# A graph network kernel: every second tile of gathered rows is copied into PSUM and the edge product is added to it there

## The chip, the cores and the metric

The kernel runs on one core of one Trainium2 chip. The metric is the device time of one execution in microseconds (us). A core has five engines with a queue of instructions each: TensorE (PE in the rows; its weight loads are PEld), VectorE (DVE), ScalarE (ACT), GpSimd (POOL) and SyncE (SP), which issues the plain DMA transfers. The engines meet only at semaphores: an instruction that waits holds back everything behind it on its engine.

## What is computed

Two layers of message passing over the same graph of 1250 nodes and 21250 edges, sorted by destination, with 512 features. What matters here is the edge part of each layer:

```python
# layer 0, edge attributes 64 wide
msg  = relu(x[src] + edge_attr @ W_e + b_e)
aggr = segment_sum(msg, dst, num_segments=N)
# layer 1, edge attributes 128 wide
m_in = concatenate([h[src], edge_attr], axis=1)
m    = relu(m_in @ W1.T + b1)
agg  = segment_sum(m, dst)        # @ W2.T + deg * b2 follow on the nodes
```

Layer 0 then has a two-layer perceptron with batch norms over the nodes, layer 1 a gated unit; both end in a layer norm. In layer 1 the node half of `W1` is applied once per node into a table, so that both layers gather ready rows and add an edge product.

## The kernel before

The edges are cut into 167 tiles of 128, in chunks of 4 tiles (one load of edge attributes) and groups of 12 tiles (one window of 128 destination nodes in which the edges of the group fall). One tile passes through the engines in this way, with L the layer and t = u the tile (`JOIN` is 1):

- GpSimd, `gather` (line 415): an indirect DMA fetches the 128 source rows of 512 floats (256 KB) into `raw`, a ring of `RAW` = 8 buffers. The buffer is free when VectorE has made the low part of tile t - 8. The first 12 tiles of layer 0 read `x` itself; later ones read `xb_dram`, x plus the bias, which VectorE makes in five pieces (`make_xb`) and SyncE writes out.
- TensorE, `edge_product` (line 510): two passes in layer 0 and three in layer 1 (the numbers are split into a high and a low part of reduced precision) give the edge product in one of `EDGE_BANKS` = 4 banks of PSUM.
- VectorE, `add_products` (line 1030): `raw` = bank + `raw`.
- ScalarE, `message_high` (line 819): Relu of `raw`, rounded, into `msg_hi`, a ring of `MSG` = 4.
- VectorE, `low_messages` (line 1018): max(`raw`, 0) - `msg_hi` into `msg_lo`, two tiles after the add.
- TensorE, `sum_product` (lines 525, 526): the one-hot matrix `hot` of the destinations times both parts, summed over a group in one of two sum banks, four tiles after the edge product. In layer 1 also the degrees (line 539).

Per chunk, ScalarE copies the attributes, rounded (`high_features`, line 794), VectorE makes their low part (`low_features`, line 949) and the one-hots (`one_hots`, line 1010). Per group, ScalarE copies the sum bank out (`copy_window`, line 794), TensorE transposes it into `turn_bank` (line 550) and VectorE adds it into `agg` (`add_window`, line 1044; degrees at line 1050).

The order on each engine is that of a loop written out by hand, `edges(L)`, one for each engine. ScalarE's loop has the features ahead of the message, the message being the only work of a tile:

```python
while chunk < min(CHUNKS, chunks_in(u + 1) + 1):
    high_features(L, chunk)
    chunk += 1
...
if u < UNITS:
    message_high(L, u)
```

VectorE's loop has for each u: the add of tile u, the low part of tile u - 2, and in every fourth u the low features of a later chunk and the one-hots of the next. `leftover(L)` treats edges outside their window; there are none in these inputs. Ahead of layer 0's loop the ten blocks of x are also transposed on TensorE (line 562) and scaled by ScalarE into `agg`, one block per tile.

## Time and profile before

| | us |
|---|---|
| median of 3 runs | 978.73 |
| lowest, highest | 976.2, 987.15 |
| the profiled execution, its time | 971.74 |
| its span in the trace | 969.9 |
| VectorE busy | 758.9 (78%) |
| TensorE busy | 814.6 (84%) |
| GpSimd busy | 396.6 (41%) |
| ScalarE busy | 367.3 (38%) |

The page cuts the span into 40 slices of 24 us and gives the busy share of each in tenths, 9 being 90% or more:

```profile
PE   4977777777777999979688878888888999999993
DVE  5899999999997992458789999999998535435255
ACT  2444544554454441321245544555554221111122
POOL 3466666666660100011577767767772000000001
```

Layer 0's edge stage goes from about 13 to 300 us, layer 1's from about 490 to 750; between and behind them lie the node products, where TensorE is full. A row that times one instruction gives its start, its length, engine, line, operation, output and inputs; in square brackets stands how long the engine was idle ahead of it and what ended that.

### The profile page before, as it was taken

The page shows a single profiled execution, that of the slowest core. Times are in us where ns is not written, and L with a number is a line of the kernel's source. Part 1 is how long each engine was busy: PE and PEld are TensorE (multiplying, and loading weights), DVE is VectorE, ACT ScalarE, POOL GpSimd, SP SyncE. Part 2 cuts the span into 40 slices and gives each one's busy share as a digit, 9 for nine tenths or more (in the row PEclk, how much of TensorE's full clock was granted, in tenths as well). Part 3 has the DMA queues.
Part 4 walks back from the last instruction along what each step waited for, and adds up shares of the span by engine and source line. Part 5 has one row for each costly group of instructions (what it writes and reads, how often), then busy time and mean ns, then how long its engine had stood idle before and what let it go on. Part 6 is the DMA issues. An engine that isn't in the chain of part 4 may idle for free.

```text
span 969.9 us, 11501 instructions
## 1 busy us (share of the span) xinstructions
PE 814.6 (84%) x3686; PEld 618.6 (64%) x3686; DVE 758.9 (78%) x1326; ACT 367.3 (38%) x597; POOL 396.6 (41%) x381
## 2 busy tenths in 40 slices
PE   4977777777777999979688878888888999999993
PEld 2534444444445999968456656666665789899893
DVE  5899999999997992458789999999998535435255
ACT  2444544554454441321245544555554221111122
POOL 3466666666660100011577767767772000000001
PEclk9999999999998999979889999999999999999997
DMA  8678777767780004003666667677663011010011
GB/s 281 216 246 232 203 207 204 202 202 206 206 266 17 1 1 174 1 2 127 204 193 199 201 200 217 199 213 207 207 196 112 9 65 67 1 66 1 1 44 63
DMA packets 50758, 137.21 MB, mean 141 GB/s; under 512 B 8256, under 2 KB 8512, under 8 KB 50311
## 3 DMA queue, kind: packets, MB, share of 16 engines
q0 software_dynamic: 26720, 87.58, 31.0%
q1 hardware_dynamic: 23974, 48.86, 15.4%
q8 instruction: 31, 0.51, 0.2%
...
## 4 chain that ended last, share of the span: by engine, by line
PE 41%; DVE 39%; issue 13%; DMA 2%; ACT 1%; POOL 1%; DVEq 1%; SPq 0%; POOLq 0%; ACTq 0%
PE banks L486 33%; DVE raw L1030 14%; DVE msg_lo L1018 13%; PE banks L510 4%; DVE hot L1010 3%; DVE attr_lo L949 2%; DVE agg L1044 2%; DMA raw<-xb_dram,src_sb 2%; DVE attr_hl L949 1%; PE banks L525 1%; DVE stats L1158 1%; PE banks L526 1%; PE banks L562 1%; DVEq L1034 1%; DVE last L1318 1%
## 5 line engine op out<-in xcount | busy, mean ns | idle before, releaser
L819 ACT ACTIVATE msg_hi<-raw 128x512 fp32r<-128x512 f32 x334 | 211.1, 632 | 282.5 <-DVE raw L1030 188.5
L1030 DVE TENSOR_TENSOR raw<-banks,raw 128x512 f32<-128x512 f32 x334 | 227.3, 681 | 18.7 <-PE banks L510 11.8
L1018 DVE SCALAR_TENSOR_TENSOR msg_lo<-raw,msg_hi 128x512 fp32r<-128x512 f32 x334 | 227.1, 681 | 0.1
L415 POOL DMA_INDIRECT raw<-table_dram,src_sb x167 | 193.4, 1158 | 81.3 <-issue 60.2
L525 PE MATMUL banks<-msg_hi,hot 128*128 128x512 f32 x334 | 153.8, 461 | 80.4 <-DVE msg_lo L1018 65.8
L415 POOL DMA_INDIRECT raw<-xb_dram,src_sb x155 | 163.3, 1053 | 93.0 <-DVE msg_lo L1018 47.4
L525 PEld LDWEIGHTS banks<-msg_hi,hot 128*128 128x128 f32 x334 | 63.1, 189 | 168.4 <-DVE msg_lo L1018 123.4
L437 POOL TENSOR_TENSOR moments<-moments,minus_half 128x1 f32<-128x1 f32 x32 | 20.4, 636 | 317.2 <-DVE moments L1164 317.2
L526 PE MATMUL banks<-msg_lo,hot 128*128 128x512 f32 x334 | 132.8, 398 | 0.0
L510 PE MATMUL banks<-V1e_hi,attr_hi 128*128 128x512 f32 x167 | 70.4, 422 | 7.5 <-DVE attr_lo L949 7.5
L510 PE MATMUL banks<-We_hi,attr_hl 128*128 128x512 f32 x167 | 69.4, 416 | 8.4 <-DVE attr_hl L949 8.4
L510 PE MATMUL banks<-We_lo,attr_hl 128*128 128x512 f32 x167 | 67.8, 406 | 0.0
L526 PEld LDWEIGHTS banks<-msg_lo,hot 128*128 128x128 f32 x334 | 63.9, 191 | 5.2
L510 PE MATMUL banks<-V1e_lo,attr_hi 128*128 128x512 f32 x167 | 66.8, 400 | 0.0
L510 PE MATMUL banks<-V1e_hi,attr_lo 128*128 128x512 f32 x167 | 66.7, 399 | 0.0
L1010 DVE TENSOR_TENSOR hot<-iota_f,in_window 128x512 fp32r<-128x512 f32 x84 | 57.3, 682 | 1.3
L486 PE MATMUL banks<-x_hi,Wg_hi 128*128 128x512 f32 (+2 forms) x144 | 50.7, 352 | 0.4 <-issue 0.4
L486 PE MATMUL banks<-m_lo,Wg_hi 128*128 128x512 f32 (+2 forms) x144 | 50.9, 353 | 0.0
L486 PE MATMUL banks<-x_lo,Wg_hi 128*128 128x512 f32 (+2 forms) x144 | 50.9, 353 | 0.0
L486 PE MATMUL banks<-x_hi,Wg_lo 128*128 128x512 f32 (+2 forms) x144 | 50.8, 353 | 0.0
L486 PE MATMUL banks<-m_hi,Wg_lo 128*128 128x512 f32 (+2 forms) x144 | 50.8, 353 | 0.0
L486 PE MATMUL banks<-m_hi,Wg_hi 128*128 128x512 f32 (+2 forms) x144 | 50.8, 353 | 0.0
...
## 6 DMA issues: line engine op xcount, KB each, us to landing
...
raw<-table_dram,src_sb POOLq DMA_INDIRECT x167
x_in<-in_x SPq DMA_DIRECT2D x5, 512.0 KB, 12.6
xb_dram<-xb SPq DMA_DIRECT2D x5, 512.0 KB, 4.2
...
```

The lines of the kernel that those rows point to most:

```text
L415: pool.indirect_dma_start(raw[L][:, t % RAW, :], None, table, bass.IndirectOffsetOnAxis(ap=src_sb[:, t:t + 1], axis=0)).then_inc(gathered[ ...
L437: nc.gpsimd.tensor_tensor(moments[:, slot * 4 + 2:slot * 4 + 3], moments[:, slot * 4 + 1:slot * 4 + 2], minus_half[:, 0:1], ALU.pow).then_ ...
L486: mm = nc.tensor.matmul(acc, a, b, start=start and i == 0, stop=stop and i == len(passes) - 1)
L510: mm = nc.tensor.matmul(acc, features, W, start=n == 0, stop=n == len(passes) - 1)
L525: nc.tensor.matmul(acc, h, msg_hi[L][:, t % MSG, :], start=start, stop=False)
L526: mm = nc.tensor.matmul(acc, h, msg_lo[L][:, t % MSG, :], start=False, stop=stop)
L819: nc.scalar.activation(msg_hi[L][:, a:a + len(tiles), :], raw[L][:, b:b + len(tiles), :], ACT.Relu).then_inc(relued[L], 1)
L949: return nc.vector.tensor_tensor(to, value, high.bitcast(F32), ALU.subtract)
L1010: nc.vector.tensor_tensor(hot[L][:, c % HOT, 0:len(tiles), :], nodes, own, ALU.is_equal).then_inc(hot_ready[L], 1)
L1018: nc.vector.scalar_tensor_tensor(msg_lo[L][:, a:a + len(tiles), :], raw[L][:, b:b + len(tiles), :], 0.0, msg_hi[L][:, a:a + len(tiles), :] ...
L1030: nc.vector.tensor_tensor(rows, banks[:, a:a + len(tiles), :], rows, ALU.add).then_inc(added[L], 1)
L1044: nc.vector.tensor_tensor(here, feature_major(turn_bank), here, ALU.add).then_inc(window_added[L], 1)
```

## The change

A step j is now two tiles, 2j and 2j + 1. Even tiles go as before, over two banks. For an odd tile ScalarE copies the gathered rows into one of three other banks (`place`), TensorE adds the edge product onto them there (its first pass has no start flag), ScalarE takes the Relu out of that bank and VectorE the low part. To make TensorE add and not overwrite, one matmul with the start flag is done in each of the three banks ahead of the loop (`prime`). Behind `place`, the row buffer of an odd tile is free.

The transposes of a window go back into its own sum bank, whose `turn_bank` is thereby free. `MSG` grows from 4 to 6, and `msg_lo`, `hot`, `sums` and `table_sb` lie elsewhere. The ten blocks of x are transposed two per step over two banks; `make_xb` runs once per step, so once per two tiles. On ScalarE, the features of a chunk come behind the messages of the step.

Blank lines are left out of the diff:

```diff
-JOIN = 1
...
-RAW, EDGE_BANKS, MSG, HOT, RING = 8, 4, 4, 3, 3
-LOW_LAG, SUM_LAG = 2 // JOIN, 4 // JOIN
+RAW, ADD_BANKS, PLACE_BANKS, MSG, HOT, RING = 8, 2, 3, 6, 3, 3
+SUM_LAG = 2
...
-COPY_AFTER, TURN_AFTER, ADD_AFTER = 0, 1, 2
+COPY_AFTER, TURN_AFTER, ADD_AFTER = 0, 1, 1
...
-        turn_bank, degree_bank = bank[6], bank[7]
+        add_bank, place_bank = bank[2:4], [bank[0], bank[1], bank[6]]
+        degree_bank = bank[7]
+        start_bank = [bank[5], bank[7]]
...
+        def edge_bank(t):
+            i = t // 2
+            return place_bank[i % PLACE_BANKS] if odd(t) else add_bank[i % ADD_BANKS]
...
-                wait(pool, low[L], -(-(t - RAW + 1) // JOIN))
+                if t >= RAW and odd(t):
+                    pool.wait_ge(placed[L], (t - RAW) // 2 + 1)
+                elif t >= RAW:
+                    pool.wait_ge(low[L], t - RAW + 1)
...
-            def edge_product(L, u):
...
+            def edge_product(L, t):
+                i, c, ks = t // 2, t // CHUNK, slice(t % CHUNK * P, (t % CHUNK + 1) * P)
+                if t % CHUNK == 0:
+                    pe.wait_ge(attr_split[L], c + 1)
+                if odd(t):
+                    pe.wait_ge(placed[L], i + 1)
+                else:
...
+                for n, (features, W) in enumerate(passes):
+                    mm = nc.tensor.matmul(edge_bank(t), features, W, start=n == 0 and not odd(t),
+                                          stop=n == len(passes) - 1, skip_group_check=odd(t))
                 mm.then_inc(add_mm[L], 1)
...
+            def prime(L):
+                pe.wait_ge((be_split, vb2_split)[L], 1)
+                for b in place_bank:
+                    mm = nc.tensor.matmul(b, ones_row[:, :], (be_hi, v_b2_hl)[L][0:1, :], start=True, stop=True)
+                mm.then_inc(primed[L], 1)
...
-            def message_high(L, u):
-                tiles = unit_tiles(u)
-                act.wait_ge(added[L], u + 1)
-                wait(act, summed[L], u - MSG // JOIN + 1)
-                a, b = tiles.start % MSG, tiles.start % RAW
-                nc.scalar.activation(msg_hi[L][:, a:a + len(tiles), :], raw[L][:, b:b + len(tiles), :],
+            def place(L, t):
+                i = t // 2
+                wait_gathered(act, L, t)
+                if i == 0:
+                    act.wait_ge(primed[L], 1)
+                elif i >= PLACE_BANKS:
+                    act.wait_ge(low[L], t - 2 * PLACE_BANKS + 1)
+                copy(edge_bank(t), raw[L][:, t % RAW, :]).then_inc(placed[L], 1)
+            def message_high(L, t):
+                if odd(t):
+                    act.wait_ge(add_mm[L], t + 1)
+                else:
+                    act.wait_ge(added[L], t // 2 + 1)
+                wait(act, summed[L], t - MSG + 1)
+                nc.scalar.activation(msg_hi[L][:, t % MSG, :], edge_bank(t) if odd(t) else raw[L][:, t % RAW, :],
                                      ACT.Relu).then_inc(relued[L], 1)
...
+                place(L, 1)
                 chunk = 2
-                for u in range(UNITS + SUM_LAG + COPY_AFTER):
-                    while chunk < min(CHUNKS, chunks_in(u + 1) + 1):
+                for j in range(STEPS + SUM_LAG + COPY_AFTER):
+                    if 0 < j <= STEPS and 2 * j - 1 < TILES:
+                        message_high(L, 2 * j - 1)
+                    if 2 * j + 3 < TILES:
+                        place(L, 2 * j + 3)
+                    if 2 * j < TILES:
+                        message_high(L, 2 * j)
+                    if L == 0:
+                        for b in step_tiles(j):
+                            if b < BLOCKS:
+                                start_sums(b)
+                    while chunk < min(CHUNKS, chunks_in(j + 1) + 1):
                         high_features(L, chunk)
                         chunk += 1
-                    if L == 0:
-                        for b in range(u * JOIN, min(BLOCKS, (u + 1) * JOIN)):
-                            start_sums(b)
-                    if u < UNITS:
-                        message_high(L, u)
                     for g in range(GROUPS):
-                        if last_unit(g) + SUM_LAG + COPY_AFTER == u:
+                        if last_step(g) + SUM_LAG + COPY_AFTER == j:
...
-            def low_messages(L, u):
-                tiles = unit_tiles(u)
-                dve.wait_ge(relued[L], u + 1)
-                a, b = tiles.start % MSG, tiles.start % RAW
-                nc.vector.scalar_tensor_tensor(msg_lo[L][:, a:a + len(tiles), :], raw[L][:, b:b + len(tiles), :], 0.0,
-                                               msg_hi[L][:, a:a + len(tiles), :].bitcast(F32), ALU.max,
+            def low_message(L, t):
+                dve.wait_ge(relued[L], t + 1)
+                nc.vector.scalar_tensor_tensor(msg_lo[L][:, t % MSG, :], edge_bank(t) if odd(t) else raw[L][:, t % RAW, :], 0.0,
+                                               msg_hi[L][:, t % MSG, :].bitcast(F32), ALU.max,
                                                ALU.subtract).then_inc(low[L], 1)
-            def add_products(L, u):
-                tiles = unit_tiles(u)
-                for t in tiles:
-                    wait_gathered(dve, L, t)
-                dve.wait_ge(add_mm[L], u + 1)
-                a, b = tiles.start % EDGE_BANKS, tiles.start % RAW
-                rows = raw[L][:, b:b + len(tiles), :]
-                nc.vector.tensor_tensor(rows, banks[:, a:a + len(tiles), :], rows, ALU.add).then_inc(added[L], 1)
+            def add_product(L, t):
+                wait_gathered(dve, L, t)
+                dve.wait_ge(add_mm[L], t + 1)
+                nc.vector.tensor_tensor(raw[L][:, t % RAW, :], edge_bank(t), raw[L][:, t % RAW, :],
+                                        ALU.add).then_inc(added[L], 1)
...
-                for u in range(UNITS + SUM_LAG + ADD_AFTER):
-                    if u < UNITS:
-                        add_products(L, u)
-                    if L == 0 and u == 8:
-                        count_left()
-                    if L == 0 and u == 16:
-                        left_flag()
-                    if L == 0 and u * JOIN < XQ:
-                        for q in range(u * JOIN, min(XQ, (u + 1) * JOIN)):
-                            make_xb(q)
-                    if 0 <= u - LOW_LAG < UNITS:
-                        low_messages(L, u - LOW_LAG)
-                    while chunk < min(CHUNKS, chunks_in(u + 1) + 1):
+                for j in range(STEPS + SUM_LAG + ADD_AFTER + 1):
+                    if j < STEPS:
+                        add_product(L, 2 * j)
+                    if L == 0 and j < XQ:
+                        make_xb(j)
+                    for t in (2 * j - 2, 2 * j - 1):
+                        if 0 <= t < TILES:
+                            low_message(L, t)
+                    while chunk < min(CHUNKS, chunks_in(j + 1) + 1):
                         low_features(L, chunk)
                         chunk += 1
-                    while hots < min(CHUNKS, chunks_in(u + 1)):
+                    while hots < min(CHUNKS, chunks_in(j + 1)):
                         one_hots(L, hots)
                         hots += 1
+                    if L == 0 and j == 6:
+                        count_left()
+                    if L == 0 and j == 10:
+                        left_flag()
                     for g in range(GROUPS):
-                        if last_unit(g) + SUM_LAG + ADD_AFTER == u:
+                        if last_step(g) + SUM_LAG + ADD_AFTER == j:
```

On ScalarE, in layer 0's steady part, the program had for eight tiles (`banks` is PSUM; `added0` comes from VectorE's adds, `summed0` and `add_mm0` from TensorE, `attr_in0` from the loads):

```order
L794 ACTIVATE attr_hl<-attr_sb 128x512 [waits add_mm0,attr_in0_0]
L819 ACTIVATE msg_hi_96<-raw_89 128x512 [waits summed0,added0] x4
L794 ACTIVATE attr_hl<-attr_sb 128x512 [waits add_mm0,attr_in0_1]
L819 ACTIVATE msg_hi_96<-raw_89 128x512 [waits summed0,added0] x4
L794 ACTIVATE sums_102<-banks 128x512 [waits window_turned0,summed0]
```

And for four tiles of it, two steps with the first of the next, it has now:

```order
L858 ACTIVATE msg_hi_96<-banks 128x512 [waits summed0,add_mm0]
L821 ACTIVATE banks<-raw_89 128x512 [waits low0,gathered0_3]
L858 ACTIVATE msg_hi_96<-raw_89 128x512 [waits summed0,added0]
L821 ACTIVATE attr_hl<-attr_sb 128x512 [waits add_mm0,attr_in0_0]
L858 ACTIVATE msg_hi_96<-banks 128x512 [waits summed0,add_mm0]
L821 ACTIVATE banks<-raw_89 128x512 [waits low0,gathered0_5]
L858 ACTIVATE msg_hi_96<-raw_89 128x512 [waits summed0,added0]
L858 ACTIVATE msg_hi_96<-banks 128x512 [waits summed0,add_mm0]
```

The feature copy (`attr_hl`) stood alone between the messages of four tiles. It now stands behind a copy into `banks` that waits for the gather (`gathered0_3`: the fourth of the ring's eight buffers, a tile of number 4k + 3) and the Relu of an even tile.

On VectorE, before, one group of four tiles in layer 0:

```order
L949 TENSOR_TENSOR attr_hl<-attr_sb,attr_hl 64x512 [waits attr_high0]
L1010 TENSOR_TENSOR hot_100<-iota_f,in_window 128x512 [waits summed0]
L1030 TENSOR_TENSOR raw_89<-banks,raw_89 128x512 [waits add_mm0,gathered0_5]
L1018 SCALAR_TENSOR_TENSOR msg_lo_98<-raw_89,msg_hi_96 128x512 [waits relued0]
L1030 TENSOR_TENSOR raw_89<-banks,raw_89 128x512 [waits add_mm0,gathered0_6]
L1018 SCALAR_TENSOR_TENSOR msg_lo_98<-raw_89,msg_hi_96 128x512 [waits relued0]
L1030 TENSOR_TENSOR raw_89<-banks,raw_89 128x512 [waits add_mm0,gathered0_7]
L1018 SCALAR_TENSOR_TENSOR msg_lo_98<-raw_89,msg_hi_96 128x512 [waits relued0]
L1030 TENSOR_TENSOR raw_89<-banks,raw_89 128x512 [waits add_mm0,gathered0_0]
L1018 SCALAR_TENSOR_TENSOR msg_lo_98<-raw_89,msg_hi_96 128x512 [waits relued0]
```

Now, four tiles again:

```order
L1070 TENSOR_TENSOR raw_89<-banks,raw_89 128x512 [waits add_mm0,gathered0_6]
L1062 SCALAR_TENSOR_TENSOR msg_lo_98<-raw_89,msg_hi_96 128x512 [waits relued0]
L1062 SCALAR_TENSOR_TENSOR msg_lo_98<-banks,msg_hi_96 128x512 [waits relued0]
L1070 TENSOR_TENSOR raw_89<-banks,raw_89 128x512 [waits add_mm0,gathered0_0]
L1062 SCALAR_TENSOR_TENSOR msg_lo_98<-raw_89,msg_hi_96 128x512 [waits relued0]
L1062 SCALAR_TENSOR_TENSOR msg_lo_98<-banks,msg_hi_96 128x512 [waits relued0]
L994 TENSOR_TENSOR attr_hl<-attr_sb,attr_hl 64x512 [waits attr_high0]
L1056 TENSOR_TENSOR hot_100<-iota_f,in_window 128x512 [waits summed0]
```

Two adds (with their waits for the gathers) are gone; two of the four low parts read `banks` in place of `raw`; the wait of the low feature part for `attr_high0` stands where it stood, behind the low parts.

On GpSimd, the gathers at the start of layer 0, before:

```order
L445 AFFINE_SELECT ident<-ident 128x128 [waits pool_consts]
L415 DMA raw_89<-in_x,src_sb 128x512 [waits src_in]
L415 DMA raw_89<-in_x,src_sb 128x512 x7
L415 DMA raw_89<-in_x,src_sb 128x512 [waits low0] x4
L415 DMA raw_89<-xb_dram,src_sb 128x512 [waits low0,xb_out] x155
```

Now:

```order
L429 DMA raw_89<-in_x,src_sb 128x512 x7
L429 DMA raw_89<-in_x,src_sb 128x512 [waits low0]
L429 DMA raw_89<-in_x,src_sb 128x512 [waits placed0]
L429 DMA raw_89<-in_x,src_sb 128x512 [waits low0]
L429 DMA raw_89<-in_x,src_sb 128x512 [waits placed0]
L429 DMA raw_89<-xb_dram,src_sb 128x512 [waits low0,xb_out]
L429 DMA raw_89<-xb_dram,src_sb 128x512 [waits placed0,xb_out]
L429 DMA raw_89<-xb_dram,src_sb 128x512 [waits low0,xb_out]
```

The gather of an odd tile waits for `placed0`, a copy of ScalarE, and that of an even one for `low0`, a low part of VectorE, as all did before.

## Rows read from the trace of the kernel before

**Rows 1.** The page, section 1: busy us, share of the span, instructions.

```profile
PE 814.6 (84%) x3686; PEld 618.6 (64%) x3686; DVE 758.9 (78%) x1326; ACT 367.3 (38%) x597; POOL 396.6 (41%) x381
```

**Rows 2.** Stages, `core 0` (from:to, length, busy us by engine, granted clock, DMA share, GB/s).

```profile
150.00:200.00 50.00, 37.92 (x138) 22.28 (x137) 49.50 (x81) 24.74 (x42) 33.13 (x32) 1.00 0.71 204
600.00:650.00 50.00, 43.04 (x204) 31.08 (x204) 50.00 (x86) 25.23 (x43) 37.22 (x32) 1.00 0.71 209
```

**Rows 3.** Line 1030 alone (the adds) in 200 us of each layer; same columns.

```profile
60.00:260.00 200.00, 84.08 (x123) 0.99 0.73 212
500.00:700.00 200.00, 84.95 (x126) 1.00 0.70 208
```

**Rows 4.** VectorE in order of time: start, us, instruction; layer 0, then layer 1.

```profile
61.00 0.69 DVE L949 TENSOR_TENSOR attr_hl<-attr_sb,attr_hl 64x512 fp32r<-64x512 f32 x1
61.72 0.69 DVE L1010 TENSOR_TENSOR hot<-iota_f,in_window 128x512 fp32r<-128x512 f32 x1
62.33 0.69 DVE L1030 TENSOR_TENSOR raw<-banks,raw 128x512 f32<-128x512 f32 x1
62.93 0.68 DVE L1018 SCALAR_TENSOR_TENSOR msg_lo<-raw,msg_hi 128x512 fp32r<-128x512 f32 x1
...
622.64 0.68 DVE L1044 TENSOR_TENSOR agg<-banks,agg 128x512 f32 x1
623.24 0.27 DVE L1050 TENSOR_TENSOR deg_r<-banks,deg_r 2x128 f32 x1
623.44 0.67 DVE L1030 TENSOR_TENSOR raw<-banks,raw 128x512 f32<-128x512 f32 x1
```

**Rows 5.** Groups of instructions, forms apart: count, busy, mean ns, idle before and releasers.

```profile
L1030 DVE TENSOR_TENSOR raw<-banks,raw 128x512 f32<-128x512 f32 x334 | 227.3, 681 | 18.7 <-PE banks L510 11.8 <-DMA raw<-table_dram,src_sb 5.0 <-DMA raw<-xb_dram,src_sb 1.8
```

**Rows 6.** Waits: engine, line, what for, us in total, times, longest.

```profile
POOL raw L415 <- DVE msg_lo L1018: 72.4, 58, 11.7
```

**Rows 7.** ScalarE in order of time, and VectorE behind it at 303.

```profile
52.31 0.63 ACT L819 ACTIVATE msg_hi<-raw 128x512 fp32r<-128x512 f32 x1 [0.57 <-DVE raw L1030]
52.85 0.58 ACT L794 ACTIVATE sums<-banks 128x512 f32<-128x512 f32 x1
53.33 0.62 ACT L794 ACTIVATE attr_hl<-attr_sb 128x512 fp32r<-128x512 f32 x1
...
302.48 1.67 ACT L794 ACTIVATE h_hi<-agg 128x512 fp32r<-128x512 f32 x3 [1.80 <-DVEq L1146]
...
303.14 1.29 DVE L949 TENSOR_TENSOR h_lo<-agg,h_hi 128x512 fp32r<-128x512 f32 x2 [0.92 <-ACT h_hi L794]
```

**Rows 8.** The chain that ended last, three of its DMA pieces: start, us, what.

```profile
65.94 8.18 DMA raw<-xb_dram,src_sb
...
274.04 6.75 DMA raw<-xb_dram,src_sb
...
487.19 3.42 DMA raw<-table_dram,src_sb
```

**Rows 9.** GpSimd in order of time.

```profile
64.36 1.27 POOL L415 DMA_INDIRECT raw<-xb_dram,src_sb  x1 [1.13 <-DVE msg_lo L1018]
65.94 0.95 POOL L415 DMA_INDIRECT raw<-xb_dram,src_sb  x1 [0.30 <-issue]
67.19 0.95 POOL L415 DMA_INDIRECT raw<-xb_dram,src_sb  x1 [0.30 <-issue]
```

**Rows 10.** Groups of instructions of GpSimd.

```profile
L415 POOL DMA_INDIRECT raw<-table_dram,src_sb x167 | 193.4, 1158 | 81.3 <-issue 60.2 <-DMA table_dram<-table_sb 13.3 <-DVE msg_lo L1018 7.7
L415 POOL DMA_INDIRECT raw<-xb_dram,src_sb x155 | 163.3, 1053 | 93.0 <-DVE msg_lo L1018 47.4 <-issue 45.5
```

**Rows 11.** VectorE at the start of layer 0; DMA issues (KB each, us to landing).

```profile
38.10 0.69 DVE L1030 TENSOR_TENSOR raw<-banks,raw 128x512 f32<-128x512 f32 x1 [0.88 <-PE banks L510]
...
47.16 0.68 DVE L1018 SCALAR_TENSOR_TENSOR msg_lo<-raw,msg_hi 128x512 fp32r<-128x512 f32 x1
...
xb_dram<-xb SPq DMA_DIRECT2D x5, 512.0 KB, 4.2
```

143 lines of the change are left out of this document (70 added, 73 removed).

## Prediction

> **What bounds the kernel now.** I read the page's first line, then the table by stage, then who waits for whom, then single instructions. The whole span hides the bound: TensorE is busy 84% of it and VectorE 78% [rows 1]. In both edge stages VectorE is busy 49.5 to 50.0 of 50 us, TensorE 37.9 and 43.0, GpSimd 33 to 37, ScalarE 25, the DMA engines 0.71 [rows 2]. So the edge stages, some 545 of 969.9 us, go at VectorE's pace; the 425 us around them don't contain the changed code. 123 adds in 200 us of layer 0 and 126 in 200 us of layer 1 [rows 3] make 1.63 and 1.59 us per tile. VectorE starts an instruction every 0.60 us (low feature part and one-hot: 0.72 in layer 0), each lasting 0.69 [rows 4]. Four tiles take 4 adds, 4 low parts, 1 feature part, 1 one-hot: 10 x 0.60 = 6.0, plus 0.24 and a third of a window add (0.60; with the degree add 0.80 [rows 4]): 6.4 and 6.3, which is the measured pace. The reader is to see also that VectorE stood idle before its 334 adds for only 18.7 us, 6.8 of them for gathers [rows 5]: gathers have slack now. GpSimd does wait for the low parts, 72.4 us in 58 waits [rows 6]: the ring of 8 row buffers holds it back, harmlessly so far.
>
> **What the change removes.** One add of two: VectorE has 8 instructions per four tiles instead of 10, naturally 4.8 + 0.24 + 0.20 = 5.24 us in layer 0 and 4.8 + 0.27 = 5.07 in layer 1, that is 1.31 and 1.27 per tile. If nothing else bound, 0.32 x 150 tiles in each layer (those outside start and drain) = 48 + 48 us would go.
>
> **What it adds.** ScalarE gets two copies per four tiles: 7.3 instructions at a pace of 0.48 to 0.54 [rows 7] = 3.8 us, room enough in itself. A copy into PSUM is not in this trace; from 0.48 (out of PSUM) to 0.54 (SBUF to SBUF) it is hardly open, I take 0.52. TensorE gets 6 priming matmuls, at times when it waits for features anyway: nothing; were that cover gone, six of TensorE's 37.92 / 138 = 0.27 us each [rows 2], 1.6 us. The bank turns and the changed window banks wait for work of 12 tiles earlier: nothing.
>
> **What it moves, which decides.** I count a step as two tiles, 2j and 2j+1. ScalarE's copy for tile 2j+3 stands ahead of the Relu of tile 2j, and at every even j the high half of the next features stands behind that Relu (order of ScalarE, above). VectorE waits for this high half in the same step, where before it was copied ahead of the message. So a late gather of tile 2j+3 stops copy, Relu, features, and VectorE. And the gather is late by construction: GpSimd issues in order; gather 2j+2 must wait for the low part of tile 2j-6, made in step j-2, and gather 2j+3 stands behind it, though its own buffer is long free. Before, a gather had six tiles of VectorE's work (9.6 us) until its add; now the odd one has less than two steps.
>
> I follow one round, from VectorE's feature part in step 0 to that in step 4, eight tiles:
> - feature part, one-hot, add of tile 2, low part of tile 0 and its end: 0.60 x 3 + 0.69 = 2.49 [rows 4];
> - from that end to the start of the gather of tile 8: the low part that starts at 62.93 ends at 63.61, the gather starts at 64.36 after 0.70 of "issue": 0.75 [rows 4, 8, 9];
> - gathers 9, 10 and 11 start 1.58, 1.25 and 1.25 after one another [rows 9] (the low part of tile 2, for gather 10, ends 4.3 into the round, before GpSimd is free at 6.1: no added wait): 4.08;
> - landing of gather 11, counted from its start: L;
> - ScalarE: copy 0.52 with 0.05 of wake-up, Relu of tile 8 0.54, features until VectorE starts: 303.14 - 302.48 = 0.66 [rows 7]: 1.77.
>
> Sum 9.09 + L. Layer 0 adds 0.24 (two one-hot and feature pairs are dearer) and a window add every third time, 0.20: 9.53 + L. Layer 1 adds 0.27 for windows, and its gathers last 1158 ns on average where layer 0's take 1053 and an undisturbed one 950 [rows 9, 10]; of 3 x 0.2 I take half: 9.66 + L.
>
> **L** shows three times in the chain: 3.42 at layer 1's start, when the queues carry little else, 6.75 and 8.18 in bursts (the latter beside the 2 MB of weights) [rows 8]. They are the worst of the chain, so the bulk lies near the low one; I take 3.8, with 3.42 and 4.8 as bounds. Then layer 0 needs 13.33 / 8 = 1.67 us per tile, layer 1 13.46 / 8 = 1.68. Against now: +0.04 x 150 = +6 and +0.09 x 155 = +14.
>
> **Start of layer 0.** The sums x + bias are now made one per step and not one per tile: the fifth stands behind the add of tile 8 (now at 38.10, the place of the fifth then: about 40). Its write-out takes 4.2 us [rows 11], gathers 12 and 13 start at about 45 and 46.6, 13 lands at 50.4, and the Relu and low part of tile 10 come behind it: 51.6 in place of 47.16 [rows 11]. I take +3, bounds 0 and 6. **Bursts:** a landing of 8.18 or 6.75 cost nearly nothing before and now goes into the round nearly whole, 4.4 + 3.0 less 1.8 already paid: +5.
>
> **Sum:** 6 + 14 + 3 + 5 = +28. The profiled execution took 971.7 us (span 969.9), 7 below the runs' median of 978.7. So 1000 in its own terms, 1007 as a median.
>
> **Two rules of the Trainium skill.** The rows give an add, which reads PSUM, and a low part, which reads SBUF alone, the same pace of 0.60 and a length of 0.69 and 0.68 [rows 4]. The Trainium skill ("VectorE: DVE Perf Modes", The TRN2 errata) gives a VectorE instruction with a PSUM source 62 cycles more than one from SBUF; it would speak against the change, since the odd low part now reads PSUM. By the row this costs nothing; by the page it would be an estimated 0.065 us per odd tile, 10 us over the kernel, and only if VectorE bound. The trace does not agree with it here. Second, the rows show gathers held beyond 950 ns, more in layer 1 [rows 9, 10]. The Trainium skill ("SBUF — State Buffer", on the shared port pair) has GpSimd contend with VectorE instructions that have two SBUF inputs; the odd low part then has only one. By that rule layer 1's 0.3 in the round would partly go: 6 us less. No row decides it.
>
> **Rivals.**
> - *VectorE or GpSimd binds, faster.* The features' wait would have to be hidden: the round 9.53 + L must come under eight tiles of the next bound. For VectorE that is 8 x 1.31 = 10.5, L under 1.0; for GpSimd at 1.053 + 0.30 = 1.35 per tile in layer 0 (1.158 + 0.30 = 1.46 in layer 1 [rows 9, 10]) L under 1.3. The smallest row is 3.42. It wins only if my order of waits is wrong, for instance if GpSimd or ScalarE runs further ahead than I see. With VectorE bound 971.7 - 96 + 3 + 7 = 886; with GpSimd bound (-0.28 x 150, -0.13 x 155, +3, +7) 920. For it: VectorE is the bound now and loses a fifth of its work. Chance 0.19 with everything between 965 and these.
> - *No change.* L = 3.42 throughout and no longer gathers in layer 1: 12.95 / 8 = 1.62 and 12.78 / 8 = 1.60, with small losses at the start: 972 to 978, as a median 979 to 988. Near my value; chance 0.21.
> - *My forecast*, the round binds with L 3.5 to 4.8: 985 to 1045, chance 0.60. At L = 4.8 the layers need 1.79 and 1.81: +24 + 34 + 8 = 1038, median 1045. For it speaks that every term has a row; against it that the round is only 3 to 6% longer than today's pace, and 0.5 us in L moves the time by 0.5 / 8 x 305 = 19 us.
>
> TensorE is no rival: 43.0 of 50 us busy at 1.59 per tile in layer 1 [rows 2] is 1.37 at most, with a granted clock of 1.00, the higher level; it keeps all its work, so I expect no other clock.
>
> **Chances.** About 1% (10 us) is what a measurement of this kernel can tell from none. Faster 0.19, within 0.21, slower 0.60. The range leaves out the far part of the faster case (below 962) and landings above 4.8.
>
> **What would show it.** Right: VectorE busy about 78% in the edge stages and idle ahead of the feature part (every fourth tile), released by ScalarE; ScalarE idle ahead of its PSUM copy, released by the gather's DMA; GpSimd's gathers at 1.67 us per tile. Wrong: VectorE still over 95% busy (then it is faster by up to 90 us), GpSimd without waits at 1.3 to 1.45 per tile, or VectorE idle ahead of an add for TensorE. The copy into PSUM should have a pace near 0.5 us, the start should be 3 to 5 us later at tile 12.

## The result, and the profile of the changed kernel

The changed kernel takes 1014.5 us (median of four runs, 1012.1 to 1017.7) where the kernel before took 978.8 in the same comparison (976.2 to 987.2): a ratio of 1.037, 95% interval 1.032 to 1.041. It is slower by 3.7%. The forecast was 1007 us with a range of 962 to 1045, and slower as the likeliest sign. The profiled execution of the changed kernel took 1012.1 us, its span 1010.3; the forecast in those terms was 1000.

The page of the changed kernel, its first line and section 1 (busy us, share of the span, instructions), and from section 5 five groups (line, engine, operation, count, busy, mean ns, idle ahead of it and who ended most of it). They answer [rows 1], [rows 5] and [rows 10]:

```profile
span 1010.3 us, 11479 instructions
PE 830.6 (82%) x3692; PEld 638.4 (63%) x3692; DVE 664.2 (66%) x1160; ACT 434.3 (43%) x763; POOL 360.6 (36%) x381
...
L429 POOL DMA_INDIRECT raw<-table_dram,src_sb x167 | 169.0, 1012 | 121.5 <-DVE msg_lo L1062 67.6
L429 POOL DMA_INDIRECT raw<-xb_dram,src_sb x155 | 152.0, 981 | 132.9 <-DVE msg_lo L1062 86.9
L821 ACT ACTIVATE banks<-raw 128x512 f32<-128x512 f32 x166 | 99.9, 602 | 226.5 <-DMA raw<-table_dram,src_sb 120.5
...
L1070 DVE TENSOR_TENSOR raw<-banks,raw 128x512 f32<-128x512 f32 x168 | 114.3, 680 | 19.7 <-PE banks L524 13.2
...
L1062 DVE SCALAR_TENSOR_TENSOR msg_lo<-raw,msg_hi 128x512 fp32r<-128x512 f32 x168 | 114.7, 683 | 15.2 <-ACT msg_hi L858 9.8
...
L1062 DVE SCALAR_TENSOR_TENSOR msg_lo<-banks,msg_hi 128x512 fp32r<-128x512 f32 x166 | 113.2, 682 | 0.9 <-ACT msg_hi L858 0.6
...
L994 DVE TENSOR_TENSOR attr_hl<-attr_sb,attr_hl 64x512 fp32r<-64x512 f32 x42 | 29.1, 694 | 62.2 <-ACT attr_hl L821 38.7
L994 DVE TENSOR_TENSOR attr_lo<-attr_sb,attr_hi 128x512 fp32r<-128x512 f32 x42 | 29.0, 693 | 57.8 <-ACT attr_hi L821 38.6
```

VectorE did lose its work: 664 us busy where it had 759, 168 adds in place of 334. But its idle time grew by more than that, from 211 to 346 us. Most of the growth stands in one place: 62.2 + 57.8 = 120 us ahead of the low half of the edge features (line 994), where before there were 1.3 us in layer 0 (the row below) and 0.0 in layer 1. It waits there for the high half from ScalarE (line 821). The profile names ScalarE for 77 us of the 120 and nobody ("issue") for 42; in each of those 21 cases too, VectorE starts 0.64 to 0.66 us after ScalarE's feature copy has started, as in the others. ScalarE in turn stood idle for 226.5 us ahead of its new PSUM copy, waiting for gathered rows. And the gathers stood idle for 254 us, 154 of it waiting for low parts, line 1062. That is the whole circle, read from one page. The row from before:

```profile
L949 DVE TENSOR_TENSOR attr_hl<-attr_sb,attr_hl 64x512 fp32r<-64x512 f32 x42 | 28.9, 691 | 1.3
```

The stages of the changed kernel (from:to, length, busy us by engine with counts, granted clock, DMA share, GB/s), the same stretches as in [rows 2]:

```profile
core 0: us, PE busy (x) PEld busy (x) DVE busy (x) ACT busy (x) POOL busy (x), PEclk, DMA share, GB/s
150.00:200.00 50.00, 36.20 (x123) 22.86 (x122) 37.29 (x61) 28.30 (x53) 28.56 (x30) 0.89 0.70 198
600.00:650.00 50.00, 41.97 (x192) 29.90 (x191) 38.88 (x65) 30.05 (x56) 30.97 (x32) 1.00 0.66 197
```

VectorE is busy 37.3 and 38.9 of 50 us, where [rows 2] had 49.5 and 50.0. No engine is full any more: the stage is bound by a chain of waits. The adds of line 1070 in 200 us of each layer (60 to 260, 500 to 700) were 57 and 58, two tiles for each: 1.75 us per tile in layer 0 and 1.72 in layer 1, against 1.63 and 1.59 of [rows 3]. The second figure is not a steady pace: layer 1's first add stands at 501 us here and at 475 before, so this stretch holds the slow start of the layer. Taken tile by tile, from the start times of the adds (us), the two kernels compare like this:

| | before | changed | later by |
|---|---|---|---|
| layer 0, add of tile 20 | 59.68 | 66.28 | 6.6 |
| layer 0, add of tile 166 | 296.76 | 322.37 | 25.6 |
| layer 1, first add | 475.13 | 501.07 | 25.9 |
| layer 1, add of tile 166 | 742.27 | 782.62 | 40.35 |
| pace, tiles 20 to 160, layer 0 / layer 1 | 1.62 / 1.59 | 1.77 / 1.67 | |

The span is 40.4 us longer, so these rows hold all of it: 6.6 us at the start, 19.0 in the rest of layer 0, 0.3 between the layers and 14.4 in layer 1.

The waits of the whole execution (engine, line, what for: us in total, times, longest), which answer [rows 6]:

```profile
POOL raw L429 <- DVE msg_lo L1062: 170.1, 92, 11.7
ACT banks L821 <- DMA raw<-table_dram,src_sb: 120.5, 78, 13.3
ACT banks L821 <- DMA raw<-xb_dram,src_sb: 98.4, 57, 7.8
```

GpSimd's wait for low parts more than doubled, 72.4 to 170.1 us, and it is no longer harmless: 78 of the 83 PSUM copies in layer 1 now start at the moment their rows land.

The round itself can be read in order of time. First the chain that ended last, in layer 0 (start, us, what):

```profile
218.72 1.41 POOL raw L429
220.13 0.30 issue
220.43 3.98 DMA raw<-xb_dram,src_sb
224.41 0.02 issue
224.43 0.02 ACT banks L821
...
224.97 0.61 ACT msg_hi L858
225.58 0.53 ACT attr_hl L821
226.11 0.02 issue
226.13 0.04 DVE attr_hl L994
```

Then VectorE around the same feature part (start, us, instruction, idle ahead of it):

```profile
222.96 0.68 DVE L1062 SCALAR_TENSOR_TENSOR msg_lo<-banks,msg_hi 128x512 fp32r<-128x512 f32 x1
226.13 0.69 DVE L994 TENSOR_TENSOR attr_hl<-attr_sb,attr_hl 64x512 fp32r<-64x512 f32 x1 [2.49 <-ACT attr_hl L821]
226.85 0.75 DVE L1056 TENSOR_TENSOR hot<-iota_f,in_window 128x512 fp32r<-128x512 f32 x1
```

The gather starts at 220.43 and lands 3.98 us later, the PSUM copy starts at 224.43, the Relu at 224.97, the features at 225.49, and VectorE gets going at 226.13: 1.70 us from the copy's start to VectorE, where the forecast had 1.77. VectorE had been idle for 2.49 us, with the low parts behind it that would free the next row buffers.

### The profile page after: what moved, and what is told of

It reads as the page before. It is cut to its first block, busy times and chain, and to the rows that moved or that the text cites. A ratio compares the mean times of both kernels' runs of the same rounds, so it can differ in the third digit from the quotient of the medians.

```text
span 1010.3 us, 11479 instructions
## 1 busy us (share of the span) xinstructions
PE 830.6 (82%) x3692; PEld 638.4 (63%) x3692; DVE 664.2 (66%) x1160; ACT 434.3 (43%) x763; POOL 360.6 (36%) x381
## 4 chain that ended last, share of the span: by engine, by line
PE 40%; DVE 18%; issue 17%; DMA 13%; POOL 6%; ACT 4%; DVEq 1%; POOLq 0%; SPq 0%; ACTq 0%
PE banks L500 31%; DVE msg_lo L1062 7%; DMA raw<-xb_dram,src_sb 7%; POOL raw L429 6%; DMA raw<-table_dram,src_sb 6%; PE banks L524 4%; DVE raw L1070 3%; DVE hot L1056 2%; ACT msg_hi L858 2%; PE banks L548 1%; PE banks L549 1%; DVE agg L1085 1%; DVE stats L1199 1%; ACT attr_hi L821 1%; PE banks L586 1%
## 5 line engine op out<-in xcount | busy, mean ns | idle before, releaser
L429 POOL DMA_INDIRECT raw<-table_dram,src_sb x167 | 169.0, 1012 | 121.5 <-DVE msg_lo L1062 67.6
L821 ACT ACTIVATE banks<-raw 128x512 f32<-128x512 f32 x166 | 99.9, 602 | 226.5 <-DMA raw<-table_dram,src_sb 120.5
L548 PE MATMUL banks<-msg_hi,hot 128*128 128x512 f32 x334 | 143.9, 431 | 10.2 <-DVE msg_lo L1062 10.1
L1070 DVE TENSOR_TENSOR raw<-banks,raw 128x512 f32<-128x512 f32 x168 | 114.3, 680 | 19.7 <-PE banks L524 13.2
L1062 DVE SCALAR_TENSOR_TENSOR msg_lo<-raw,msg_hi 128x512 fp32r<-128x512 f32 x168 | 114.7, 683 | 15.2 <-ACT msg_hi L858 9.8
L858 ACT ACTIVATE msg_hi<-raw 128x512 fp32r<-128x512 f32 x168 | 104.2, 620 | 36.8 <-DVE raw L1070 34.8
L1062 DVE SCALAR_TENSOR_TENSOR msg_lo<-banks,msg_hi 128x512 fp32r<-128x512 f32 x166 | 113.2, 682 | 0.9 <-ACT msg_hi L858 0.6
L524 PEld LDWEIGHTS banks<-We_hi,attr_hl 128*128 128x128 f32 x167 | 36.4, 218 | 108.2 <-issue 53.0
L858 ACT ACTIVATE msg_hi<-banks 128x512 fp32r<-128x512 f32 x166 | 96.4, 581 | 0.0
L524 PEld LDWEIGHTS banks<-V1e_hi,attr_hi 128*128 128x128 f32 x167 | 32.1, 192 | 63.9 <-ACT banks L821 42.1
L994 DVE TENSOR_TENSOR attr_hl<-attr_sb,attr_hl 64x512 fp32r<-64x512 f32 x42 | 29.1, 694 | 62.2 <-ACT attr_hl L821 38.7
L994 DVE TENSOR_TENSOR attr_lo<-attr_sb,attr_hi 128x512 fp32r<-128x512 f32 x42 | 29.0, 693 | 57.8 <-ACT attr_hi L821 38.6
```

The costliest lines, as they stand in the source:

```text
L429: pool.indirect_dma_start(raw[L][:, t % RAW, :], None, table, bass.IndirectOffsetOnAxis(ap=src_sb[:, t:t + 1], axis=0)).then_inc(gathered[ ...
L524: mm = nc.tensor.matmul(edge_bank(t), features, W, start=n == 0 and not odd(t), stop=n == len(passes) - 1, skip_group_check=odd(t))
L548: nc.tensor.matmul(acc, h, msg_hi[L][:, t % MSG, :], start=start, stop=False)
L821: return nc.scalar.activation(to, of, ACT.Copy)
L858: nc.scalar.activation(msg_hi[L][:, t % MSG, :], edge_bank(t) if odd(t) else raw[L][:, t % RAW, :], ACT.Relu).then_inc(relued[L], 1)
L994: return nc.vector.tensor_tensor(to, value, high.bitcast(F32), ALU.subtract)
```

## Experiments

Three theories stood before the first four experiments. **Theory 1** is the prediction's: the round of eight tiles (low part, gather behind its even partner, landing, PSUM copy, Relu, features, VectorE) sets the pace. **Theory 2**: TensorE, whose granted clock fell to 0.88 in layer 0, costs the time. **Theory 3**: gathers can't come faster than about 1.7 us per tile, whatever the order of the waits. The table gives medians and the ratio to the kernel before, which ran beside each kernel on the same chip. The kernels came in four sessions, each on another chip: e1 to e4, e5 to e8, e9 to e11, and e12 alone.

| kernel | median us | before beside it | ratio (95%) |
|---|---|---|---|
| changed kernel | 1014.5 | 978.8 | 1.037 (1.032 to 1.041) |
| e1 features first | 951.1 | 973.2 | 0.976 (0.970 to 0.982) |
| e2 copy last | 955.0 | 973.2 | 0.983 (0.977 to 0.989) |
| e3 odd gather first | 941.2 | 973.2 | 0.967 (0.962 to 0.972) |
| e4 ring of 6 | 1275.4 (one run) | 973.2 | |
| e5 x + bias early | 1010.5 | 971.9 | 1.039 (1.032 to 1.046) |
| e6 TensorE kept busy | 1017.2 | 971.9 | 1.046 (1.040 to 1.053) |
| e7 = e2 + e3 + e5 | 907.4 | 971.9 | 0.933 (0.927 to 0.939) |
| e8 = e1 + e3 + e5 | 910.0 | 971.9 | 0.935 (0.929 to 0.941) |
| e9 e7, even low part twice | 1000.2 | 974.5 | 1.025 (1.017 to 1.033) |
| e10 e7, odd low part twice | 985.3 | 974.5 | 1.011 (1.006 to 1.017) |
| e11 = e2 + e3 | 986.7 | 974.5 | 1.011 (1.005 to 1.017) |
| e12 e11 again | 917.9 | 973.2 | 0.943 (0.936 to 0.949) |

**Cutting the round in three places.** Each of the first three kernels is the changed kernel with one piece of order moved; all work stays.

e1: ScalarE makes the high features ahead of the PSUM copy and the even Relu.

```diff
                     if 0 < j <= STEPS and 2 * j - 1 < TILES:
                         message_high(L, 2 * j - 1)
+                    while chunk < min(CHUNKS, chunks_in(j + 1) + 1):
+                        high_features(L, chunk)
+                        chunk += 1
                     if 2 * j + 3 < TILES:
                         place(L, 2 * j + 3)
...
-                    while chunk < min(CHUNKS, chunks_in(j + 1) + 1):
-                        high_features(L, chunk)
-                        chunk += 1
```

> The features of a chunk are copied by ScalarE ahead of the PSUM copy and of the even tile's Relu; nothing else differs from the changed kernel (1014.5 us). Theory 1 (the round: low part, two gathers, landing, PSUM copy, Relu, features, VectorE): VectorE's idle time ahead of the feature part (120 us) goes; what is left of the round runs over three steps, end of a low part + 0.75 + 1.58 + 4.0 landing + 0.58 copy + 0.66 Relu + 0.69 low part = 8.26 us for six tiles, with unequal steps 1.42 to 1.45 per tile in place of 1.74, so 305 x 0.3 = 90 us less: 915 to 935 us. Theory 2 (TensorE at a granted clock of 0.88 in layer 0, and its waits for the PSUM copy): no change, 1005 to 1020. Theory 3 (gathers as such can't come faster than 1.7 us per tile under this order): no change, 1005 to 1020, and the idle time moves from the feature part to the low part.

e2: the PSUM copy last in ScalarE's step.

```diff
-                    if 2 * j + 3 < TILES:
-                        place(L, 2 * j + 3)
                     if 2 * j < TILES:
                         message_high(L, 2 * j)
...
                         high_features(L, chunk)
                         chunk += 1
+                    if 2 * j + 3 < TILES:
+                        place(L, 2 * j + 3)
```

> The copy into PSUM stands last in ScalarE's step, behind the even tile's Relu and the features. Theory 1: a late gather then holds back neither; it holds the odd tile's Relu of the next step, whose low part comes 0.6 us later than the even one: 7.7 us in three steps, near VectorE's own 1.3 per tile, so 1.36 to 1.42 per tile: 900 to 925 us, a little below the run with only the features moved. Theories 2 and 3: 1005 to 1020.

e3: GpSimd issues the odd gather, whose buffer is free earlier, ahead of its even partner.

```diff
-                for t in range(TILES):
+                late = [t for i in range(RAW // 2, STEPS) for t in (2 * i + 1, 2 * i) if t < TILES]
+                for t in list(range(RAW)) + late:
                     gather(L, t)
```

> GpSimd issues the gather of an odd tile ahead of that of its even partner, nothing else differs from the changed kernel. Theory 1: the odd gather then stands behind a low part that is made one step earlier and behind one gather less; the round for eight tiles is 2.49 + 0.75 + 1.58 + 4.0 + 1.77 = 10.6 us, 1.32 per tile, about VectorE's own pace: 1.35 to 1.42 per tile, 900 to 925 us. Theory 2: 1005 to 1020. Theory 3: 1005 to 1020.

Each of the three gives back more than the whole loss: 951, 955 and 941 us, all below the kernel before. Theory 3 falls with that: gathers came at 200 / 133 = 1.50 us per tile. Theory 2 had expected no gain either, since no matmul was taken away; but the clock rose with the pace (0.98 in e1), and it takes e6, below, to tell the one from the other. The sizes missed: the expectations said 900 to 935. What e1 looks like in 200 us of layer 0, first the stage, then three of its groups:

```profile
60.00:260.00 200.00, 146.50 (x576) 100.44 (x575) 177.41 (x282) 129.30 (x242) 137.50 (x133) 0.98 0.77 227
```

```profile
L429 POOL DMA_INDIRECT raw<-xb_dram,src_sb x133 | 138.1, 1038 | 62.7 <-DVE msg_lo L1061 34.1 <-issue 25.6 <-ACT banks L821 3.0
L821 ACT ACTIVATE banks<-raw 128x512 f32<-128x512 f32 x66 | 39.7, 602 | 68.3 <-DMA raw<-xb_dram,src_sb 67.9
L993 DVE TENSOR_TENSOR attr_hl<-attr_sb,attr_hl 64x512 fp32r<-64x512 f32 x33 | 22.7, 688 | 1.0
```

The wait ahead of the features is gone (1.0 us), as meant, but the copy still waits for landings (67.9) and the gathers for low parts (34.1). e3 in the same stretch keeps another wait, the features' (19.6 of it for ScalarE):

```profile
L995 DVE TENSOR_TENSOR attr_hl<-attr_sb,attr_hl 64x512 fp32r<-64x512 f32 x33 | 22.7, 689 | 20.3 <-ACT attr_hl L822 19.6
```

So each cut leaves a shorter round of the same sort, which was not priced. That became theory 4, below.

**Closing the round over fewer tiles.** e4 has six row buffers in place of eight. The odd gather then stands behind a low part of the step before, so that a round, nearly as long as the old one, serves four tiles and not eight.

```diff
-RAW, ADD_BANKS, PLACE_BANKS, MSG, HOT, RING = 8, 2, 3, 6, 3, 3
+RAW, ADD_BANKS, PLACE_BANKS, MSG, HOT, RING = 6, 2, 3, 6, 3, 3
```

> The ring of row buffers has 6 in place of 8. Theory 1: the odd gather stands behind a low part of the step before, so the round covers four tiles and not eight: 2.49 + 0.75 + 1.58 + 4.0 + 1.77 + 0.44 = 11.0 us for four tiles, 2.76 per tile in place of 1.74: 305 x 1.0 more, about 1320 us. Theories 2 and 3: gathers and engines work as before, at most some waits more: 1015 to 1060.

1275 us, from one execution; the reading rests on its waits. In layer 0 there are 40 adds in 200 us, 2.5 us per tile (2.76 expected), and VectorE stands idle for 97.4 of them ahead of the features, on average 4.9 us ahead of each of the 20:

```profile
L994 DVE TENSOR_TENSOR attr_hl<-attr_sb,attr_hl 64x512 fp32r<-64x512 f32 x20 | 13.8, 689 | 97.4 <-ACT attr_hl L821 97.4
```

Four tiles take 10.2 us (tiles 20 to 160) where 11.0 were expected of the round. With two buffers fewer the kernel is 26% slower, and GpSimd issues a gather every 2.6 us where it has shown a gather every 1.3.

**The start, and the clock.** e5 makes x + bias at the places by tile that it had before.

```diff
-                    if L == 0 and j < XQ:
-                        make_xb(j)
+                    if L == 0:
+                        for q in range(2 * j, min(XQ, 2 * j + 2)):
+                            make_xb(q)
```

> The changed kernel, with VectorE making two blocks of x + bias per step instead of one, until all five are done (so at the places by tile that they had before the change). Theory 1 has a term for the start: tile 12 is gathered from these sums, and in the changed kernel 16 tiles are added in the first 60 us instead of 21, about 8 us lost, where the prediction took 3. If the late sums are the cause: 1006 to 1009 us in place of 1014.5, gather 12 starts about 3 us earlier than 45.25 us, and 18 or 19 tiles are added by 60 us. If the start is lost to the round itself (the features behind the late PSUM copy), the time stays within 3 us of 1014.5 and still about 16 tiles are added by 60 us.

GpSimd at the start of layer 0, gather 12 in each; the changed kernel, then e5:

```profile
45.25 0.95 POOL L429 DMA_INDIRECT raw<-xb_dram,src_sb  x1 [12.29 <-DMA xb_dram<-xb]
```

```profile
37.74 0.95 POOL L429 DMA_INDIRECT raw<-xb_dram,src_sb  x1 [4.63 <-DVE msg_lo L1062]
...
54.80 0.95 POOL L429 DMA_INDIRECT raw<-xb_dram,src_sb  x1 [2.81 <-DVE msg_lo L1062]
```

Gather 12 starts 7.5 us earlier (3 were expected). The round takes back a part of it, and only a part: gather 20 starts at 54.80 and in the changed kernel at 60.67, a lead of 5.9 us. The add of tile 20 is 5.3 us earlier (60.97 and 66.28), layer 1 starts 5.4 us earlier, and the profiled span is 4.5 us shorter (1005.8 and 1010.3). In the first 60 us, 20 tiles are added in place of 16. So neither expectation came true as written: the late sums do cause most of the loss at the start, and a lead of 4 to 6 us stays to the end, but the ratios, 1.039 and 1.037, can't tell an effect of that size.

e6 keeps TensorE busy with two extra matmuls per step in layer 0.

```diff
+                    if L == 0 and 16 <= j < STEPS:
+                        for _ in range(2):
+                            nc.tensor.matmul(bank[7], We_hi[:, 0:P], We_hi[:, :], start=True, stop=True)
```

> The changed kernel, with two more 128x128x512 matmuls per step on TensorE in layer 0, from step 16 on, into a PSUM bank that nobody reads then, from operands that are always there; about 0.45 us of every 3.5 us step. They only keep TensorE busy. Its granted clock in 60 to 260 us was 0.88. Theory 2 (the lower clock costs the time): the clock returns to 0.95 to 1.00 and layer 0 gets faster than 1.75 us per tile, 1.60 to 1.65: 1000 us or less. Theory 1 (the round over gather, PSUM copy, Relu and features holds no matmul that is late): the clock rises too and the pace stays 1.73 to 1.77, time 1011 to 1019.

```profile
60.00:260.00 200.00, 150.97 (x592) 107.28 (x590) 148.44 (x239) 111.88 (x208) 112.16 (x115) 0.96 0.67 196
```

The clock rose from 0.88 to 0.96 over the stretch, the pace stayed (57 adds, VectorE 148.4 against 148.9 us busy), and the time is 1017. Theory 2 is out for layer 0: there the lower clock goes with TensorE's waiting, and giving most of it back gains nothing.

**Cutting both rounds.** Theory 4: in e2 the odd gather still stands behind its even partner, in e3 the features still stand behind the copy; with both mended the next bound is VectorE or GpSimd. Theory 5: the gathers hold 1.43 whatever the order. e7 is e2 + e3 + e5, e8 is e1 + e3 + e5 (the diffs above together).

> Three edits on the changed kernel at once: GpSimd issues the gather of the odd tile ahead of its even partner, ScalarE's PSUM copy stands last in its step, behind Relus and features, and x + bias is made two blocks per step. Alone, the first gave 941 us and the second 955, both at 1.43 to 1.49 us per tile, where theory 1 as first priced expected 900 to 925. Theory 4: each of the two leaves another, shorter round through a late gather (the first leaves the features behind the copy; the second leaves the odd gather behind its even partner, and the copy still holds up the next odd Relu and through it the low parts that free the buffers); with both gone the next bound is VectorE, 1.31 and 1.27 per tile, or GpSimd, about 0.98 + 0.30 = 1.28 to 1.35: 895 to 915 us. Theory 5: the gathers as such (GpSimd's waits for low parts and landings under load) hold 1.43 to 1.45 whatever the order: 930 to 940.

> As the run before, but in place of the PSUM copy being last only the features are ahead of it: ScalarE does the odd Relu, the features, then the PSUM copy, then the even Relu. Theory 4: the copy of tile 2j+3 still stands ahead of the Relu of tile 2j, and now waits for a gather that was issued one place earlier; a little slower than the run before, 900 to 925 us. Theory 5: 930 to 940, like the run before.

907 and 910 us, both in theory 4's range and 6.5 to 6.7% below the kernel before. e7 by stage, and its VectorE and GpSimd groups in layer 0:

```profile
60.00:240.00 180.00, 144.22 (x573) 98.06 (x572) 171.01 (x275) 130.91 (x242) 134.25 (x131) 1.00 0.83 250
500.00:670.00 170.00, 162.29 (x781) 120.50 (x778) 160.49 (x266) 122.18 (x228) 129.90 (x124) 1.00 0.77 235
```

```profile
L429 POOL DMA_INDIRECT raw<-xb_dram,src_sb x131 | 135.1, 1031 | 46.1 <-issue 34.1 <-ACT banks L822 6.1 <-DVE msg_lo L1063 5.9
...
L1071 DVE TENSOR_TENSOR raw<-banks,raw 128x512 f32<-128x512 f32 x65 | 44.3, 682 | 5.2 <-DMA raw<-xb_dram,src_sb 5.1
```

VectorE is busy 95% of layer 0's stretch, the tiles come at 180 / 130 = 1.38 us, and GpSimd waits only 12 us of 180 for buffers; the rest is its own work, 1031 ns and 0.30 between two gathers, 1.33 per tile. So VectorE (1.31 worked out in the prediction) and GpSimd (1.33) lie almost level, and what is left is between them. e8 was expected a little slower than e7 and is not measurably so: its copy waits 49.9 us for landings in layer 0 where e7's waits 7.7, and the time hardly shows it.

**A doubled instruction, and a session that can't be compared.** e9 and e10 are e7 with one low part per step computed a second time into an unread buffer: that of the even tile (two SBUF inputs), or of the odd one (one in PSUM). e11 is e7 without e5's edit.

```diff
                 dve.wait_ge(relued[L], t + 1)
+                if odd(t) is False:
+                    wait(dve, spare[L], t // 2)
+                    nc.vector.scalar_tensor_tensor(lf_msg[L][:, :], edge_bank(t) if odd(t) else raw[L][:, t % RAW, :], 0.0,
+                                                   msg_hi[L][:, t % MSG, :].bitcast(F32), ALU.max, ALU.subtract).then_inc(spare[L], 1)
```

(e10 has True for False.)

> The kernel of 907 us (odd gather first, copy last, x + bias early) with one more VectorE instruction per step: the low part of the even tile is computed a second time, into a buffer that nobody reads. It reads two tiles from SBUF. VectorE then has 10 instructions per four tiles again, as before the change. If VectorE is what binds the kernel of 907 us: 0.30 us per tile more on 305 tiles, less the 0.07 by which that kernel is above VectorE's own 1.31: 970 to 995 us, VectorE over 97% busy. If the gathers still bind it: below 950. The second thing it tells: GpSimd's gathers took 1053 and 1158 ns (layers 0 and 1) before the change, where 6 of VectorE's 10 instructions read two tiles from SBUF; 1012 and 981 after it, with 4 of 8 and VectorE often idle. If two-input VectorE work slows the gathers, they take over 1050 and over 1130 ns here.

> As the run before, but the low part of the odd tile is computed twice: the same operation and the same length of work, with one input in PSUM and one in SBUF, so 4 of VectorE's 10 instructions read two tiles from SBUF instead of 6. Time: as the run before within 1% if a PSUM source costs VectorE nothing; with 62 cycles more on each instruction from PSUM it would be about 10 us slower. Gathers: if the pair of SBUF inputs is what slows them, about 1030 and 1060 ns here, less than in the run before; if only VectorE's busy share counts, the same as there.

> The kernel of 907 us without the edit on x + bias. In the changed kernel that edit alone moved gather 12 forward by 7.5 us, and the round took most of it back before 55 us: 1010.5 against 1014.5. If the round hid it, it shows here, where the round is gone: the first 60 us hold 16 tiles in place of 20, and the time is 911 to 915. If the start is held by something else: 905 to 909.

e11 gave 987 us, where 911 to 915 were expected at most, and it was slower than e7 in layer 1 too, where the two programs are the same. So the same kernel was run once more as e12, in another session and on another chip.

> The kernel that gave 987 us (odd gather first, copy last, no edit on x + bias), once more in a call of its own. It was slower than the kernel of 907 us in layer 1 too, where the two programs are the same, and there VectorE waited up to 5 us for single gathered rows. If the edit on x + bias is the cause (through what it starts): a ratio to before of 1.00 to 1.02 again. If the two calls aren't comparable, because gathers landed later in that one: a ratio of 0.93 to 0.945 here, 905 to 917 us.

It gave 918 us there. So the edit on x + bias is not the cause; something in that session was. Where the round is gone the edit does show: the add of tile 20 starts at 69.8 us in e12 and at 61.1 in e7, 8.7 us of the 10.5 between their spans. Layer 1 of e11, then of e12:

```profile
500.00:670.00 170.00, 146.89 (x648) 107.67 (x646) 133.55 (x220) 101.25 (x188) 104.56 (x102) 0.92 0.66 196
```

```profile
500.00:670.00 170.00, 161.96 (x777) 120.38 (x775) 161.48 (x268) 122.52 (x227) 130.94 (x124) 1.00 0.78 238
```

And what e11's VectorE waited for in 500 to 700 us, which has no counterpart in e12 ("remote" means that the profile found no releaser):

```profile
DVE raw L1071 <- remote: 21.9, 6, 5.0
```

For tiles 40, 76, 100, 116 and 136 of layer 1 it took 9.0 to 9.2 us from the gather's start to the add, where the quick ones took 3.6. This looks like late rows, and it is not. An add waits for two things, its gathered rows and its edge product. Tile 76 in e11, its gather, VectorE's wait for the product (line 1070, an instruction of its own ahead of the add), and the add:

```profile
599.77 0.95 POOL L429 DMA_INDIRECT raw<-table_dram,src_sb  x1 [0.30 <-issue]
```

```profile
L1070 DVEq EVENT_SEMAPHORE  x1: 21/21/21, 608.8 to 608.8; - x1
```

```profile
608.90 0.69 DVE L1071 TENSOR_TENSOR raw<-banks,raw 128x512 f32<-128x512 f32 x1 [4.31 <-remote]
```

The last landing of its rows that the trace holds stands at 603.15, 3.4 us after the gather's start. The wait for the product ended at 608.83, although the product's last matmul is recorded as ended at 604.87. The same holds for all eight adds of layer 1 that waited for "remote" by more than 1.5 us. Where the profile names the gather instead, that wait had ended 2 us and more before the add (e12: 79.5 for an add at 83.2). Instructions that wait for no row stood in the same way, such as ScalarE's copy of the sum bank (7.9 us over e11). So what came late are TensorE's semaphore signals. In e11, e9 and e10 the trace has signals of edge products 1 to 3.6 us behind the last product recorded as ended; in the edge stages of e7 and e12 it has none. What held them in that session is not settled, nor how much of e11's 69 us they make and how much the lower clock (0.92) that came with the stalls. The kernel before ran at 974.5 beside e11, as elsewhere. That its slack hides such stalls is likely but not shown: no trace of it from that session is on record.

For e9 and e10 this means that only their own session can be compared with, where e11 stands at 987. Even that is no clean base: e11 lacks the edit on x + bias, its add of tile 20 starts at 71.4 us and theirs at 62.6, and it has more of the late signals. By the medians a doubled VectorE instruction costs nothing beside it in e10 (985) and 1.4% in e9 (1000); by the spans, with the 8.8 us of the start taken out of e11, an estimated 7 and 24 us. The forecast of 970 to 995 from a VectorE bound, made for e9, is missed by 5 us. e10 was to lie within 1% of e9, or above it, and lies 1.5% below. What still reads plainly is layer 0 of e9, a single stretch: 62 adds in 200 us, 1.61 us per tile with 10 VectorE instructions per four tiles, which is the pace of the kernel before [rows 3], and VectorE full again:

```profile
60.00:260.00 200.00, 141.36 (x537) 96.50 (x536) 196.89 (x319) 122.16 (x227) 126.85 (x123) 0.96 0.75 212
```

So in layer 0, with e7's order and two more VectorE instructions per four tiles, VectorE's count of instructions does set the pace.

## Why the prediction was right, step by step

**The bound before, and what is removed.** Right. VectorE lost 95 us of busy time (759 to 664), and 8 instructions per four tiles were priced at 1.31 us per tile; e7 comes to 1.38 with that same count. One small reading was off: in [rows 4] the feature part takes 0.72 us to the next start, but the one-hot only 0.61, so the pair costs 0.12 us more than the rest in layer 0 and not 0.24, and the price by [rows 4] is 1.28.

**The mechanism.** Right, and shown from three sides: taking the features, the copy or the odd gather out of the round removes the loss (e1 to e3), and a smaller ring makes it grow (e4, one execution). Every sign that was named is in the trace: VectorE idle ahead of the feature part, released by ScalarE (120 us); ScalarE idle ahead of the PSUM copy, released by the gather (219 us of waits); a pace of 1.77 and 1.67 us per tile (1.67 and 1.68 forecast). VectorE's share in the stages came out at 74 to 78% (78 forecast).

**Term by term.** The part from PSUM copy to VectorE was 1.70 against 1.77. The landing L was the soft term. In the changed kernel, each PSUM copy that waited gives one value, its start less that of its own gather: in layer 0 a mean of 4.5 us (61 copies, median 4.0, longest 9.5), in layer 1 of 3.9 (80 copies). I had 3.8 in both, and 5 us apart for bursts. With the measured L the same sum gives (9.53 + 4.5) / 8 = 1.75 and (9.66 + 3.9) / 8 = 1.70, against 1.77 and 1.67 measured over tiles 20 to 160. So the working of the round held to 0.03 us per tile (with the one-hot put right, layer 0's sum is 1.74); layer 0 was 0.10 too low, most of it because the one number for L was taken at the low end of three rows.

**The start.** Undersized: +3 forecast, 6.6 came by the add of tile 20. Gather 12 was forecast well (about 45, it came at 45.25), but before it had come at 35.8, and what that costs was put too low. e5, which brings gather 12 forward, wins back 5.3 of the 6.6 us.

**The sum.** 28 forecast, 40 came in the span: the start 6.6 in place of 3, the rest of layer 0 19 in place of 6 + 5 for the round and the bursts, layer 1 14 in place of 14. So the miss is in layer 0's landings and in the start, and layer 1 came out as forecast. The median hid a part of it, by luck: it lay 2.4 us above the profiled execution this time, where I had added 7.

**TensorE's clock.** Wrong. I wrote that I expected no other clock; in 60 to 260 us of layer 0 it fell from 0.99 to 0.88, a mean of stretches at 2.4 and at 1.2 GHz, TensorE having become idle more often (145.5 us busy of 200, 149.1 before). By e6 it had no part in layer 0's pace; in layer 1, where 14 us were lost, it was 0.98.

**The rivals.** "VectorE or GpSimd binds" had prices that fit another kernel than the one in the diff: I put 886 and 920 for these two bounds, and e7, where both nearly bind, takes 907. The odds against it were right only for the order of waits as written; a few lines of order separate +3.7% from -6.7%.

**The two rules.** An odd low part, which reads PSUM, takes 682 ns, an even one, which reads SBUF, 683, an add 680: nothing of 62 cycles is to be seen. The Trainium skill ("VectorE: DVE Perf Modes", The TRN2 errata) gives VectorE 120 cycles beside its elements from PSUM and 58 from SBUF, so 62 more; no run here agrees, and e10, which doubles an instruction with a PSUM source, is not slower than e9 of the same session, which doubles one without. Second, the gathers: they became shorter after the change (1053 to 981 ns in layer 0, 1158 to 1012 in layer 1), but VectorE's load fell too. e9 and e10 have the same load, with 6 and 4 instructions of two SBUF inputs in ten. In 500 to 700 us:

```profile
L430 POOL DMA_INDIRECT raw<-table_dram,src_sb x116 | 142.4, 1227 | 59.5 <-issue 31.2 <-DVE msg_lo L1068 27.4 <-ACT banks L823 0.9
```

```profile
L430 POOL DMA_INDIRECT raw<-table_dram,src_sb x123 | 146.5, 1191 | 54.3 <-issue 25.9 <-ACT banks L823 19.1 <-DVE msg_lo L1068 9.3
```

1227 and 1191 ns in layer 1, in layer 0 1035 and 1049, the other way round. The Trainium skill ("SBUF — State Buffer", on the shared port pair) has a VectorE instruction with two SBUF inputs contend with a GpSimd instruction that reads SBUF. These runs show longer gathers beside a fuller VectorE in both layers and no clear effect of the kind of input; e9 was expected over 1050 and 1130 ns by that rule and shows 1035 and 1227. It stays open.
